# Inputs of a selective scan: the work of GpSimd moved to ScalarE and VectorE, with longer rings

## The reference

```
xz = x @ in_proj_w.T                       # x_in is the first half of it
xc = conv1d(x_in, conv_w, causal, 4 taps, one filter per channel) + conv_b
u = silu(xc)
x_dbl = u @ x_proj_w.T                     # 33 columns: dt_raw, Bp, Cp
dt = softplus(dt_raw @ dt_proj_w.T + dt_proj_b)
dt = clip(dt, 1e-4, 10)
...                                        # the scan takes dt, dt * u, Bp, Cp
```

## Time and profile before

| what | us |
|---|---|
| median of 3 runs (lowest, highest) | 6533.08 (6529.61, 6537.54) |
| the profiled execution: its own time | 6532.31 |
| its span in the trace | 6530.6 |

### The profile page before, as it was taken

One profiled execution on the slowest core, in us unless ns is written; L12 is line 12 of the kernel. 1 busy time (PEld: TensorE's weight loads), 2 busy tenths in 40 slices (PEclk: granted clock), 3 DMA queues, 4 the chain that ended last, 5 costly groups with the idle time before them and its releaser, 6 DMA issues. The chain is left out here.

```text
span 6530.6 us, 93690 instructions
## 1 busy us (share of the span) xinstructions
PE 5225.0 (80%) x27420; PEld 2029.7 (31%) x27420; DVE 4930.3 (75%) x10471; ACT 3779.0 (58%) x5329; POOL 1363.7 (21%) x1658
## 2 busy tenths in 40 slices
PE   6979799797979799795999644438888888877778
PEld 3333333333333333333666322201111111115555
DVE  6666675767666675766888698879999999986768
ACT  4555555555555555552444466657777777774433
POOL 0000000000000000000111244443333333334421
PEclk8989899897989899897999866655555555558999
DMA  0000000000000000001111133331111111115422
GB/s 23 1 14 1 14 1 1 14 1 14 1 14 1 14 1 1 7 1 38 42 41 42 61 117 117 111 106 44 45 45 45 44 44 45 45 39 161 156 90 71
DMA packets 198904, 273.56 MB, mean 42 GB/s; under 512 B 13989, under 2 KB 157989, under 8 KB 192454
## 3 DMA queue, kind: packets, MB, share of 16 engines
q1 hardware_dynamic: 181190, 252.90, 12.7%
q10 hardware_dynamic: 17408, 16.78, 0.7%
HBM read 151.14 MB, written 118.49 MB: 41 GB/s over the span
## 5 line engine op out<-in xcount | busy, mean ns | idle before, releaser
L644 DVE TENSOR_REDUCE at_nmax<-at_ps_t 128x1 f32<-128x512 f32 x2048 | 1321.1, 686 | 584.4 <-PE at_ps_t L344 567.1
L486 ACT ACTIVATE at_probsT<-at_ps_s 128x1024 f32<-128x1024 f32 x1024 | 1046.0, 1023 | 810.3 <-PE at_ps_s L369 810.3
L2045 DVE SCALAR_TENSOR_TENSOR sc_decayed<-sc_da,sc_state 128x256 f32<-128x256 f32 x2048 | 777.3, 425 | 141.5 <-ACT sc_da L2000 141.5
L2000 ACT ACTIVATE sc_da<-sc_da,sc_a_col 128x1024 f32<-128x1024 f32 x512 | 560.0, 1094 | 346.2 <-PE sc_da L1936 346.2
L2055 DVE CUSTOM_DVE_ANT_0 sc_state<-sc_xd,sc_decayed 128x256 f32<-128x256 f32 x2048 | 757.3, 410 | 0.0
L344 PE MATMUL at_ps_t<-at_qkT 108*128 108x512 bf16 x2048 | 711.5, 413 | 42.8 <-DVE at_nmax L644 19.4
L1912 POOL TENSOR_SCALAR sc_xd<-sc_xd 128x1024 f32<-128x1024 f32 x512 | 533.1, 1041 | 957.4 <-ACT sc_xd L2007 957.4
L1948 PE MATMUL sc_ps_du<-sc_parts,sc_sel 24*128 24x512 bf16 x1024 | 565.4, 609 | 203.5 <-ACT sc_xd L2007 203.5
L2007 ACT ACTIVATE sc_xd<-sc_ps_du,sc_bt 128x512 f32<-128x512 f32 x1024 | 651.8, 696 | 5.9 <-PE sc_ps_du L1948 5.9
L378 PE MATMUL at_ps_o<-at_probsT,at_v 128*32 128x256 f32 x8192 | 633.2, 392 | 1.2
L365 PE MATMUL at_ps_s<-at_qkT 108*128 108x512 bf16 x2048 | 624.0, 387 | 0.0
(11 more groups left out here) (308 smaller groups left out, 7983.5 us busy)
## 6 DMA issues: line engine op xcount, KB each, us to landing
dt_parts<-si_pt SPq DMA_DIRECT2D x64, 384.0 KB, 2.6
du_parts<-si_pu SPq DMA_DIRECT2D x64, 384.0 KB, 3.2
sc_parts<-dt_parts SPq DMA_DIRECT2D x128, 192.0 KB
sc_parts<-du_parts SPq DMA_DIRECT2D x128, 192.0 KB
u_tok<-si_ut SPq DMA_DIRECT2D x8, 2048.0 KB, 8.3
y<-sc_yo SPq DMA_DIRECT2D x256, 64.0 KB
so_yin<-y SPq DMA_DIRECT2D x32, 512.0 KB
so_uin<-u_tok SPq DMA_DIRECT2D x32, 512.0 KB
```

Of the source, the lines that this page charges most:

```text
L486: nc.scalar.activation(probsT[:, c % RING, :], ps_s[c % 2][:], ACT.Exp).then_inc(s_exp, 1)
L644: nc.vector.tensor_reduce(nmax[:, par, c, t:t + 1], ps_t[c][:], AX_X, ALU.max, negate=True).then_inc(s_max, 1)
L2000: nc.scalar.activation(flat, flat, ACT.Exp, scale=a_col[:]).then_inc(s_da, 1)
L2045: nc.vector.scalar_tensor_tensor(decayed[:, ch], da[q % 2][:, j % 2, ch], DECAY_MIN, state[:, (j - 1) % SRING, ch], ALU.max, ALU.mult).the ...
```

## The change

GpSimd gets no work in the phase apart from clearing the padding. The addition of one becomes an activation on ScalarE (`raised`), issued after the absolute value of the next tile. The subtractions of the first parts go to VectorE (`rests`), one tile behind `products`, and `third_parts` moves to two tiles behind. ScalarE's `split` is cut into `first_parts(t)` and `second_parts(t - 1)`. The rings of `dt`, `du`, `pt` and `pu` have four tiles instead of two, with a semaphore for each place. `acc` is gone: the convolution is done in `u` and silu in place.

```diff
+    RING = 4
+    USES = TB // RING
...
-                w, i = t % 2, b * TB + t
+                w, i = t % RING, b * TB + t
...
         @block.gpsimd
         def _(pool):
             nc.gpsimd.memset(xc[:, :, 0:PAD], 0.0).then_inc(s_zero, 1)
-            nc.gpsimd.memset(one_col[:], 1.0)
-            pool.drain()
-
-            with pool.Fori(0, B) as b:
-                for t in range(TB):
-                    pool.wait_ge(s_ex, b * TB + t + 1)
-                    nc.gpsimd.tensor_tensor(ex1[:, t], ex[:, t], one_col[:].broadcast_to([P, DI]),
-                                            ALU.add).then_inc(s_ex1, 1)
-                for t in range(TB):
-                    w, i = t % 2, b * TB + t
-                    pool.wait_ge(s_t1, i + 1)
-                    nc.gpsimd.tensor_tensor(dt[:, w], dt[:, w], pt[:, w, 0], ALU.subtract).then_inc(s_tr, 1)
-                    pool.wait_ge(s_u1, i + 1)
-                    nc.gpsimd.tensor_tensor(du[:, w], du[:, w], pu[:, w, 0], ALU.subtract).then_inc(s_ur, 1)
...
-                    nc.scalar.activation(u[:, m], acc[:, m], ACT.Silu).then_inc(s_u, 1)
+                    nc.scalar.activation(u[:, m], u[:, m], ACT.Silu).then_inc(s_u, 1)
...
+            def raised(t):
+
+                nc.scalar.activation(ex1[:, t], ex[:, t], ACT.Copy, bias=1.0).then_inc(s_ex1, 1)
+
             def exps(b, t):
 
                 act.wait_ge(s_arg, b * TB + t + 1)
                 nc.scalar.activation(ex[:, t], arg[:, t], ACT.Abs)
                 act.drain()
-                nc.scalar.activation(ex[:, t], ex[:, t], ACT.Exp, scale=-1.0).then_inc(s_ex, 1)
+                if t > 0:
+                    raised(t - 1)
+                nc.scalar.activation(ex[:, t], ex[:, t], ACT.Exp, scale=-1.0)
 
             def logs(b):
 
                 act.drain()
+                raised(TB - 1)
...
-            def split(b, t):
-                w, i = t % 2, b * TB + t
+            def first_parts(b, t):
+                w, i = t % RING, b * TB + t
                 act.wait_ge(s_du, i + 1)
-                act.wait_ge(s_stt[w], b * TB * 8 + t // 2 * 16)
-                act.wait_ge(s_std[w], b * TB * 8 + t // 2 * 16)
+                act.wait_ge(s_stt[w], (b * USES + t // RING) * 16)
+                act.wait_ge(s_std[w], (b * USES + t // RING) * 16)
                 nc.scalar.copy(pt[:, w, 0], dt[:, w]).then_inc(s_t1, 1)
                 nc.scalar.copy(pu[:, w, 0], du[:, w]).then_inc(s_u1, 1)
+
+            def second_parts(b, t):
+                w, i = t % RING, b * TB + t
                 act.wait_ge(s_tr, i + 1)
                 nc.scalar.copy(pt[:, w, 1], dt[:, w]).then_inc(s_t2, 1)
...
                 for t in range(TB):
-                    split(b - 1, t)
+                    first_parts(b - 1, t)
+                    if t >= 1:
+                        second_parts(b - 1, t - 1)
                     if t == 2:
                         bc_stored(b)
                         act.wait_ge(s_stu, 16 * b)
                     if t >= 3:
                         u_stored(b, t - 3)
+                second_parts(b - 1, TB - 1)
...
+            def rests(b, t):
+                w, i = t % RING, b * TB + t
+                dve.wait_ge(s_t1, i + 1)
+                nc.vector.tensor_tensor(dt[:, w], dt[:, w], pt[:, w, 0], ALU.subtract).then_inc(s_tr, 1)
+                dve.wait_ge(s_u1, i + 1)
+                nc.vector.tensor_tensor(du[:, w], du[:, w], pu[:, w, 0], ALU.subtract).then_inc(s_ur, 1)
+
             def third_parts(b, t):
-                w, i = t % 2, b * TB + t
+                w, i = t % RING, b * TB + t
+                dve.wait_ge(s_ur, i + 1)
                 dve.wait_ge(s_t2, i + 1)
...
-                for t in range(1, TB):
-                    products(b, t)
-                    third_parts(b, t - 1)
-                third_parts(b, TB - 1)
+                for t in range(1, TB + 2):
+                    if t < TB:
+                        products(b, t)
+                    if t <= TB:
+                        rests(b, t - 1)
+                    if t >= 2:
+                        third_parts(b, t - 2)
```

More of the change, by code:

```diff
@@ L1395, in ssm_input_phase @@
         xT = sb("xT", [P, KD, T])
-        one_col = sb("one_col", [P, 1])
         xc = sb("xc", [P, KI, PAD + T])
-        acc = sb("acc", [P, KI, T])
         u = sb("u", [P, KI, T])
@@ L1405, in ssm_input_phase @@
         lg = sb("lg", [P, TB, DI])
-        dt = sb("dt", [P, 2, DI])
-        du = sb("du", [P, 2, DI])
+        dt = sb("dt", [P, RING, DI])
+        du = sb("du", [P, RING, DI])
         ut = sb("ut", [P, TB, DI])
-        pt = sb("pt", [P, 2, PARTS, DI], BF16)
-        pu = sb("pu", [P, 2, PARTS, DI], BF16)
+        pt = sb("pt", [P, RING, PARTS, DI], BF16)
+        pu = sb("pu", [P, RING, PARTS, DI], BF16)
         ps = [psum(f"ps{n}", [P, HALF]) for n in range(8)]
@@ L1432, in ssm_input_phase @@
         s_arg = sem("softplus_arg_ready")
-        s_ex = sem("softplus_exp_ready")
         s_lg = sem("softplus_log_ready")
@@ L1448, in ssm_input_phase @@
         s_stu = sem("u_saved")
-        s_stt = [sem(f"dt_parts_saved{w}") for w in range(2)]
-        s_std = [sem(f"du_parts_saved{w}") for w in range(2)]
+        s_stt = [sem(f"dt_parts_saved{w}") for w in range(RING)]
+        s_std = [sem(f"du_parts_saved{w}") for w in range(RING)]
         x_v = x2.rearrange("b (n p) d -> p b n d", p=P)
@@ L1500, in _ @@
             for s in s_stt + s_std:
-                sp.wait_ge(s, B * TB * 8)
+                sp.wait_ge(s, B * USES * 16)
         @block.gpsimd
@@ L1668, in _ @@
             for t in range(TB):
-                split(B - 1, t)
+                first_parts(B - 1, t)
+                if t >= 1:
+                    second_parts(B - 1, t - 1)
+            second_parts(B - 1, TB - 1)
         @block.vector
@@ L1678, in conv @@
                     dve.wait_ge(s_xc, 2 * KI * b + 2 * m + 2)
-                    nc.vector.tensor_scalar(acc[:, m], xc[:, m, 0:T], cw[:, m, 0:1], cb[:, m:m + 1], ALU.mult, ALU.add)
+                    nc.vector.tensor_scalar(u[:, m], xc[:, m, 0:T], cw[:, m, 0:1], cb[:, m:m + 1], ALU.mult, ALU.add)
                     dve.drain()
                     for j in range(1, CONV):
-                        last = nc.vector.scalar_tensor_tensor(acc[:, m], xc[:, m, j:j + T], cw[:, m, j:j + 1],
-                                                              acc[:, m], ALU.mult, ALU.add)
+                        last = nc.vector.scalar_tensor_tensor(u[:, m], xc[:, m, j:j + T], cw[:, m, j:j + 1],
+                                                              u[:, m], ALU.mult, ALU.add)
                         if j < CONV - 1:
```

## The result

| | before | after |
|---|---|---|
| median us (lowest to highest, 4 runs each) | 6532.95 (6529.61 to 6537.54) | 6477.94 (6477.75 to 6483.4) |
| profiled execution: span | 6530.6 | 6476.1 |

A forecast was written before the change was run, and what follows sets the result against it. VectorE, stretched by GpSimd's rows and by waits, was taken to bound the pass. Saving 7.9 us in each of seven passes (55.2) and 2.1 in the last part, 57.3 in all, gave 6476 us, range 6464 to 6495.

The forecast's parts named there:

- What bounds: Loop pass of 81.3 us: VectorE sets the length, busy 73.1, its rows stretched beside GpSimd's, plus waits of 1.71.
- ScalarE's additions: 8 activations of 128x512 a pass on ScalarE, 0.53 us each and 0.66 for the last.
- the table rival: ACT.Copy on ScalarE needs another table: 15 loads of 1.28 us a pass, 6628; very small, slower cases 0.04 together.
- Convolutions and logarithm: Pass start: four convolutions in 19.6 us instead of 24.38, then VectorE waits 0.7 for the first logarithm.
- The stall behind the silus: After the first two tiles, VectorE waits 2.55 us for tile 0's first part, as ScalarE still has its silus.
- The tiles: Token tiles after the stall: 34.7 us on VectorE, 5.14 a tile, with no wait within them or at the end.
- The last token part: Token part after the loop: 62.4 us becomes 60.3, 2.1 saved, with no stall.
- The chain's 9.06 us: Stretch ahead of the first convolution stays 9.06 us; rival: TensorE's clock lengthens it, 6487, 0.17 with dearer ScalarE.
- dearer ScalarE: ScalarE takes 0.70 us per addition and hands over later: 11 us back, 6487; 0.17 together with the clock case.
- Slower rivals: Long rows not GpSimd's doing, 6582, or ACT.Copy wanting another table, 6628; 0.04 together.

The follow-up runs named there:

- x_ghost: The changed kernel plus GpSimd's 24 rows a pass on tiles of its own, for which nobody waits: 6565.49 us, ratio 1.0057 to the kernel before.
- x_early: The changed kernel with ScalarE making the first parts of tile 0 between the second and third silu, not behind the fourth: 6459.86 us.
- x_lag1: The changed kernel with rings of two and the third part one tile behind instead of two: 6554.75 us.
- x_lag1r4: The changed kernel with the third part one tile behind instead of two, rings of four kept: 6514.92 us.
- x_idle: The changed kernel with TensorE waiting before the last tile's transposes of u until ScalarE has made the last tile's first parts: 6476.71 us.
- x_best: x_early plus the wait of x_idle and 16 transposes of the identity behind the last tile's transposes of u: 6454.15 us.
- x_warm: The changed kernel with unread identity transposes added on TensorE, 10 behind the u transposes of tiles 4 to 6, 28 behind the last: 6470.04 us.

## Why the prediction was right

- *What bounds.* Right: all of the phase's gain stands in VectorE's rows. That the long rows are GpSimd's doing was argued from two kinds of rows; x_ghost showed it with nothing else changed: 4.2 us of the convolutions, and rows of 1.5 us in the tokens once GpSimd gets in.
- *ScalarE's additions.* 0.53 forecast and 0.53 measured from start to start (L1603, 0.63 busy); no table load more, 8 of each of three lines, so the table rival is out.
- *Convolutions and logarithm.* 20.35 us up to the first token instruction forecast, 20.29 measured.
- *The stall behind the silus.* 2.55 forecast, 2.37 measured; x_early showed it to be on the path.
- *The tiles.* Tokens 44.05 us by both. ScalarE has five instructions a tile in 2.6 us (4198.15 to 4200.75), not the six or seven that I wrote beside the same sum. The step left no wait because of two edits that I cost at nothing, and rightly in sum: x_lag1 and x_lag1r4 show that they are worth 77 us together (6554.75 to 6477.94). I had reasoned that the ring's wait is empty with four, not that it is 3.8 us with two.
- *The last token part.* 60.3 forecast, 60.2 measured.
- *The chain's 9.06 us.* The step that failed: five passes of seven had 10.8 to 11.3, so passes saved 47.7 us instead of 55.2. It was a rival, with 0.17 for itself and dearer ScalarE, at 6487. The time still came to 6478 because the rest of the program ran 4.6 us shorter in the profiled execution (0.4 ahead and 4.2 behind), by lines that are the same in both kernels. As far as the runs show that is luck: the phase itself gave 49.9 us of 57.3.
- *Slower rivals.* Both out.

Open is what decides which passes draw the long chain. It repeats between the two profiled executions of the changed kernel, yet x_lag1r4's own executions differ by 17 us (whether by the chain isn't shown; only the fastest has a trace). It isn't whether the idle stretch right before is 3.8 or 6.6 us (x_idle). Whether a stretch under 1 us would do without added work, as x_best has with it, was not run. The Trainium skill ("TensorE: Matmul & The Clock Gate", "What's actually happening") says that sustained activity releases a clock that is low by default; x_warm and x_best agree: 7.5 to 7.9 us where TensorE worked until some 1 us before the chain, 8.7 to 11.4 in all kernels where it did not (the first passes of these two apart, where the added transposes stand in the way).

## What to carry to other kernels

When an engine's rows have two lengths, lay the other engines' rows beside them before you call the work slow; taking the neighbour's work over can be cheaper than sharing. Lay them side by side in order of time: a mean of 3.1 us was one row of 30 and fifteen of 1.3. Price the hand-over places by the last producer's queue, and move one instruction of that queue ahead before you move more work. Test each part alone, and again when what it pays with is mended: the half that looked like the larger saving, the convolutions, bought nothing while it made ScalarE late, and some 19 us once x_early had mended that. The depth of a ring carried as much as the move itself.

## What the runs showed of the hardware

A GpSimd subtraction of 128x512 took 1.15 us with least company in the kernel before (L1519). Beside VectorE rows that followed without a gap, nearly all with two inputs, its first subtraction did not end before VectorE's first gap (30.2 us in each of x_ghost's eight token parts, VectorE's rows at 0.70 meanwhile). Once there had been a gap the two engines took turns, and a VectorE row came every 1.45 us instead of 0.60. So what a neighbour's row costs VectorE depends on whether VectorE's own stream has gaps for it.

TensorE's chain of 16 transposes and the first two products takes 7.5 us at a clock of 1.00 and, in the changed kernel, 9.0 to 11.3 at 0.78 to 0.59; the 16 transposes alone take 1.94 us in x_best's seventh pass and 3.65 in x_idle's long one. In x_best 16 idle transposes ahead of the chain, at most 3.6 us of an engine that had nothing to do, gave that back in six passes of seven.
